# Causal attention and the experts behind it, joined in one block, with one activation-table load moved

## The reference, cut to what matters

```python
qkv = einsum(layernorm(x), qkv_weight)                # 16 heads of 8, 4 key heads
probs = softmax(where(causal, q @ k * scale, min))    # over the 32 positions of the first axis
h = x + (probs @ v) @ proj_weight                     # "hidden_after_attn"
x2 = layernorm(h)
gate = softmax(x2 @ router_weight)                    # 8 experts, top 2 keep their probability
h_mid = gelu(x2 @ moe_w1)                             # for each expert, 256 wide
out = h + sum(weight_e * (h_mid_e @ moe_w2_e))
```

## Time and profile before

| | us |
|---|---|
| median of 3 runs | 852.64 (851.43 to 855.21) |
| the profiled execution, its own time | 857.17 |
| its span (first to last instruction) | 855.3 |
| PE busy | 720.1 (84%) |
| DVE busy | 614.5 (72%) |
| ACT busy | 418.2 (49%) |
| POOL busy | 218.1 (25%) |

### The profile page before, as it was taken

One profiled execution on the slowest core, in us unless ns is written; L12 is line 12 of the kernel. 1 busy time (PEld: TensorE's weight loads), 2 busy tenths in 40 slices (PEclk: granted clock), 3 DMA queues, 4 the chain that ended last, 5 costly groups with the idle time before them and its releaser, 6 DMA issues. The chain is left out here.

```text
span 855.3 us, 25351 instructions
## 1 busy us (share of the span) xinstructions
PE 720.1 (84%) x9696; PEld 526.7 (62%) x9696; DVE 614.5 (72%) x1802; ACT 418.2 (49%) x777; POOL 218.1 (25%) x327
## 2 busy tenths in 40 slices
PE   3459988889797999998996488778759999999997
PEld 2335555555465767776774255556537888888886
DVE  7567887877777888888872688777555666666653
ACT  3022333223243777776664356656425455554553
POOL 3344222332428133431001734331011111011100
PEclk9968999899796999999997699999969999999999
DMA  4000000041035122222200000000000000000000
GB/s 104 9 18 18 23 21 21 23 96 21 12 84 128 54 63 74 74 77 70 82 15 13 0 5 4 5 4 5 4 3 1 14 12 5 8 12 12 12 13 13
DMA packets 33078, 26.36 MB, mean 31 GB/s; under 512 B 9740, under 2 KB 29912, under 8 KB 32984
## 3 DMA queue, kind: packets, MB, share of 16 engines
q1 hardware_dynamic: 29944, 24.07, 10.7%
q10 hardware_dynamic: 3040, 0.98, 0.5%
HBM read 13.51 MB, written 7.34 MB: 24 GB/s over the span
## 5 line engine op out<-in xcount | busy, mean ns | idle before, releaser
L1964 PEld LDWEIGHTS bank<-w2r,hme 128*128 128x128 f32 x1024 | 132.6, 192 | 15.8 <-ACT hme L1909 1.4
L1964 PE MATMUL bank<-w2r,hme 128*128 128x128 f32 x1024 | 135.8, 276 | 0.0
L1909 ACT ACTIVATE hme<-bank,b 128x512 f32<-128x512 f32 x128 | 86.5, 687 | 97.7 <-PE bank L104 97.7
L1933 DVE SCALAR_TENSOR_TENSOR Xq<-bank,wgte,Xq 128x128 f32 (+1 forms) x256 | 72.1, 343 | 52.6 <-PE bank L1964 39.8
L1096 DVE TENSOR_REDUCE mx<-bank 128x4 f32<-128x512 f32 x128 | 87.9, 688 | 24.9 <-PE bank L1141 23.4
L1014 ACT ACTIVATE P<-bank 128x512 f32<-128x512 f32 x128 | 76.5, 600 | 15.3 <-PE bank L1162 14.0
L530 ACT ACTIVATE w2r<-bank 128x512 f32<-128x512 f32 x40 | 23.9, 597 | 115.4 <-PE bank L843 85.2
L1089 DVE TENSOR_SCALAR P<-P 128x512 f32<-128x512 f32 x128 | 61.3, 479 | 3.1 <-ACT P L1014 3.0
L102 PE MATMUL bank<-xTe,w 128*128 (+1 forms) x128 | 49.2, 385 | 5.4 <-PEq L1328 5.4
L1739 POOL TENSOR_SCALAR rs<-mv 128x4 f32<-128x4 f32 x8 | 1.6, 194 | 203.4 <-DVE mv L1801 203.4
L854 PE MATMUL bank<-w_raw,hm 128*128 128x128 f32 x320 | 49.1, 303 | 2.8 <-DVE X L768 2.4
(11 more groups left out here) (384 smaller groups left out, 1779.3 us busy)
## 6 DMA issues: line engine op xcount, KB each, us to landing
cross_q<-qh SPq DMA_DIRECT2D x24, 128.0 KB
Q<-cross_q SPq DMA_DIRECT2D x8, 384.0 KB, 4.1
X<-in_x SPq DMA_DIRECT2D x8, 256.0 KB, 2.8
Xq<-X SPq DMA_DIRECT2D x32, 64.0 KB
cross_k<-kh SPq DMA_DIRECT2D x16, 128.0 KB
Yq<-Y SPq DMA_DIRECT2D x32, 64.0 KB
out_x<-Xq SPq DMA_DIRECT2D x32, 64.0 KB
cload<-in_ctx SPq DMA_DIRECT2D x8, 192.0 KB, 2.6
```

The costliest lines, as they stand in the source:

```text
L1909: act.activation(hm[:, p % HR], UP[p % RING][:], ACT.Gelu_apprx_tanh, bias=b1[:, p:p + 1]).then_inc(s["gelu"], 1)
L1933: last = dve.scalar_tensor_tensor(x, Y[f % 2][:, 128 * i:128 * i + 128], w, x, ALU.mult, ALU.add)
L1964: last = pe.matmul(Y[f % 2][:, cols], hm[:, p % HR, cols], w2r[:, p], start=(p % 2 == 0 and i == 0), stop=(p % 2 == 1), skip_group_check=True)
```

## The change

The two functions `attention2` and `experts1` become one block. `experts` no longer opens a block of its own but returns five functions, which the engines call behind their part of the attention. What the barrier had guaranteed is now said by waits on semaphores of the attention (`t` is the attention's set): PE waits ahead of its first upward product for the last `at_f` (its bank 0 is read by L1552), for the last reads of the other banks, and for the last but one `at_lo`; behind the projection of group 1 it waits for the last `at_lo`. ACT gets one more activation, a gelu of one column (the half of `half2`, written to `Kc`, which nobody reads any more) behind the exponential of the first group, which brings the gelu's table load there. Nothing of what is computed changes.

```diff
-def attention2(nc, d, bank, keep, H, AT, wp, e):
+def attention2_experts(nc, d, bank, keep, H, AT, wp, out, e):
...
+        sync, gpsimd, scalar, vector, tensor = experts(bank, keep, Xq, H, AT, wp, out, e, s)
...
                 expert_root(pool, e, 0)
                 expert_sum(pool, e, Xq, H, 0)
+                gpsimd(pool)
...
                     if q == QUADS + 1:
                         expert_exp(act, e, 0)
+                        act.activation(Kc[:, 0:1], half[:, 0, 0:1], ACT.Gelu_apprx_tanh)
                 for q in range(FIRST, QUADS + 4):
                     step(q)
+                scalar(act)
...
+                vector(dve)
...
+                tensor(pe)
...
-def experts1(nc, d, bank, keep, X3, H, AT, wp, out, e):
+def experts(bank, keep, X3, H, AT, wp, out, e, t):
...
+    def gpsimd(pool):
+        pool.wait_ge(t["summed"], G)
+        pool.wait_ge(t["h_ready"], G)
...
+    def vector(dve):
+        dve.wait_ge(t["h_ready"], G)
...
+    def tensor(pe):
+        pe.wait_ge(keep["w2_in"], 16)
+        pe.wait_ge(t["at_f"], G)
+        pe.wait_ge(t["at_lo"], G - 1)
+        pe.wait_ge(t["dd_inv"], G)
+        pe.wait_ge(t["o_sb"], G)
+        pe.wait_ge(t["p_ready"], 4 * G)
+        pe.wait_ge(t["v_ready"], 4 * G)
+        pe.wait_ge(t["mT_ready"], 4 * G)
+        pe.wait_ge(s["g_in"], 1)
...
+                if nxt(g) and p == 0:
+                    expert_project(pe, e, AT, wp, PX, g + 1)
+                    if isinstance(g, int) and g == 0:
+                        pe.wait_ge(t["at_lo"], G)
...
-        attention2(nc, d, bank, keep, keep["X"], AT, wp, moe)
-        experts1(nc, d, bank, keep, keep["Xq"], keep["X"], AT, wp, out, moe)
+        attention2_experts(nc, d, bank, keep, keep["X"], AT, wp, out, moe)
```

More of the change, by code:

```diff
@@ L1326, in attention2, with _ @@
         FIRST = -12
+        sync, gpsimd, scalar, vector, tensor = experts(bank, keep, Xq, H, AT, wp, out, e, s)
         with nc.Block() as block:
+            @block.sync
+            def _(sp):
+                sync(sp)
             @block.gpsimd
@@ L1877, in late @@
         return (h, (p - lag) % NB) if cur(h) else None
[L1879 to L1927, removed]
-                else:
[L1929 to L1986, removed]
@@ new lines, in sync, with step @@
+    def sync(sp):
+        for g in range(G):
+            sp.wait_ge(s["x4_ready"], g + 1)
+            for i in range(4):
+                at = 32 * i + GB * g
+                sp.dma_start(out[:, at:at + GB, :], X3[32 * i:32 * i + 32, GB * g:GB * g + GB, :]
+                             ).then_inc(s["stored"], 16)
+        sp.wait_ge(s["stored"], 16 * 4 * G)
+    def gpsimd(pool):
+        pool.wait_ge(t["summed"], G)
+        pool.wait_ge(t["h_ready"], G)
+        def step(g):
+            for p in range(NB):
+                if nxt(g) and p == 1:
+                    expert_root(pool, e, g + 1)
+                if nxt(g) and p == 9:
+                    expert_sum(pool, e, X3, H, g + 1)
+        over_rest(pool, step, G - 1)
@@ new lines, in scalar, with step @@
+    def scalar(act):
+        def step(g):
+            for p in range(NB):
+                k = NB * g + p
+                if cur(g):
+                    act.wait_ge(s["up_psum"], k + 1)
+                    after(act, s["down_psum"], k - HR + 1)
+                    act.activation(hm[:, p % HR], UP[p % RING][:], ACT.Gelu_apprx_tanh, bias=b1[:, p:p + 1]
+                                   ).then_inc(s["gelu"], 1)
+                if nxt(g) and p == 6:
+                    expert_high(act, e, PX, g + 1)
+                if nxt(g) and p == 10:
+                    expert_exp(act, e, g + 1)
+        over_rest(act, step, G - 1)
@@ new lines, in vector, with combine, step @@
+    def vector(dve):
+        dve.wait_ge(t["h_ready"], G)
+        def combine(at):
+            if at is None:
+                return
+            g, p = at
+            f = p // 2
+            wait_alone(dve, s["down_psum"], NB * g + p + 1, s["carrier4"])
+            if f == 0:
+                wait_alone(dve, s["r_ready"], g + 1, s["carrier4"])
+            else:
+                wait_alone(dve, s["x4_step"], (NE - 1) * g + f, s["carrier4"])
+            for i in range(GB):
+                x = group(X3, g)[:, i, :]
+                w = group(wgt, g)[:, i, f:f + 1]
+                last = dve.scalar_tensor_tensor(x, Y[f % 2][:, 128 * i:128 * i + 128], w, x, ALU.mult, ALU.add)
+            last.then_inc(s["x4_ready" if f == NE - 1 else "x4_step"], 1)
+        def step(g):
+            for p in range(NB):
+                if p % 2 == 0:
+                    combine(late(g, p, LAG + 1))
+                if nxt(g):
+                    expert_prep(dve, e, H, PX, LG, g + 1, p)
+        over_rest(dve, step, G - 1)
+        for f in (NE - 2, NE - 1):
+            combine((G - 1, 2 * f + 1))
@@ L1989, in causal_tiles @@
+    return sync, gpsimd, scalar, vector, tensor
 def causal_tiles(room):
```

34 lines of the change are left out of this document (added).

## The result

The changed kernel takes 848.44 us (median of 17 runs, 845.01 to 851.87), the kernel before 853.39 (17 runs, 850.16 to 856.22). The ratio is 0.9946, with a 95% interval of 0.9929 to 0.9962: 0.54% less, give or take 0.17%, which is 4.6 us with an interval of 3.2 to 6.1 (the medians differ by 4.95). The forecast was 849.5, within a range of 846.4 to 851.4, and a gain of 3.1 us. The time lies in the range, and the gain is larger than forecast, on the edge of what was called no change.

What follows compares the result with a forecast made beforehand. PE, full through the experts to the end, was taken to bound the kernel, with the barrier's idle time ahead of it. A gain of 4.14 - 1.0 (clock) = 3.1 us from the median 852.64 gave 849.5, range 846.4 to 851.4.

Steps and rivals of the forecast that it cites:

- What bounds the kernel, and the hole: PE is full through the experts to the end; ahead, the barrier idles it 5.44 us without needing the routing's result.
- The barrier goes: 4.14 us: At the border of attention and experts, the product of p = 1 starts at 638.41 instead of 642.55, gaining 4.14 us.
- rival 6: Some wait holds PE's first product until at_lo; gain only 1.6 us, time 851.0; chance 0.05.
- The pause at `at_lo`: Behind the projection of group 1, PE stands still about 0.5 us (1.7 at full clock) for the last at_lo.
- The table load: On ACT behind the routing's exponential, the load's new place and the added gelu neither gain nor cost anything.
- rival 4: The table load delays ACT's high half and thus the wait at at_lo; 0.35 us less gain, 849.9; chance 0.03.
- The clock: 1.0 us of loss: Half clock lasts 3.4 to 6.8 us behind the at_lo pause, costing 1.0 us more, between 0.15 and 1.85.
- rival 2: The at_lo pause is too short to matter to the clock; gain 3.8 to 5.5 us, about 848.0; chance 0.20.
- What follows: DVE's norm for group 1 stays in time with at least 0.9 us of room; the shift reaches the end.
- The slower side: Loop code no longer stays loaded; reloads in six passes cost 7 to 11 us, time 856.5 to 860; chance 0.05.
- The rivals with 851.0: Gain only 1.6 us: an issue pause in the new dense stretch (chance 0.06), or first product held until at_lo (0.05).
- rival 1: The forecast itself, for the border of attention and experts: gain 2.3 to 4.0 us, 848.6 to 850.3; chance 0.43.

Runs made afterwards that it cites:

- e2_load_only: The kernel before, barrier kept, with only the added one-column gelu that brings the table load forward; ratio to the kernel before 1.0006.
- e1_no_early_load: The changed kernel without the added one-column gelu, so the table load falls back ahead of the first real gelu; ratio to the kernel before 0.9945.
- e3_at_lo_first: The changed kernel with PE's wait for the last at_lo moved ahead of its first upward product; ratio to the kernel before 0.9986.
- e6_at_lo_early: The changed kernel with the routing's comparison (steps 12 and 13) moved on DVE behind the last low half; ratio to the kernel before 0.9955.
- e7_gap_filled: The changed kernel with the routing's comparison moved behind the last low half and 6 unused matmuls on PE behind the widening; ratio to the kernel before 0.9946.
- e8_both_gaps_filled: The changed kernel with the routing's comparison moved, and unused PE matmuls, 6 ahead of the last widening and 7 behind; ratio to the kernel before 0.9949.
- e4_wait_routing: The changed kernel, without barrier, but PE waits for DVE's last routing copy ahead of its first upward product; ratio to the kernel before 0.9998.
- e9_at_lo_between: The changed kernel with only step 13 of the routing moved on DVE behind the last low half; ratio to the kernel before 0.9949.
- e11_changed_again: The changed kernel measured once more, unaltered, beside its variants on one chip; ratio to the kernel before 0.9964.
- e10_between_filled: The changed kernel with only routing step 13 moved behind the last low half, plus 6 and 7 unused PE matmuls around the widening; ratio 0.9942.
- e5_border_filled: The kernel before, barrier kept, with 42 unused matmuls of 128 columns on PE behind its last widening; ratio to the kernel before 0.9983.

## Why the prediction was right, and where it was off

**What bounds the kernel, and the hole.** Right. PE stays full from 640 to 840 us, and from the transpose to the end it is 203.8 us before and 203.7 after, so what is won at the border arrives at the end: profiles with and without the barrier differ at the transpose by 4.9 us (17.97 and 17.20 on one side; 12.73, 13.36 and 11.93 on the other; means 17.59 and 12.67), and the medians of the first measurement by 4.95.

**The barrier goes: 4.14 us.** Right in size: 4.13 between the two profiles, 4.14 between e2_load_only and e1_no_early_load (8.60 and 4.46). `at_lo` and not the waits ahead of the first product is what limits p = 1. e3_at_lo_first shows it from the other side: with the two pieces of work behind `at_lo` instead of ahead, p = 1 comes at 7.45. That is the kernel of rival 6, and its gain of 1.54 us up to p = 1 is close to the 1.6 given there. The pause at `at_lo` was to be 0.5 us. The profile counts 0.27, by a modelled end; by the starts, which the prediction went by, it is 2.99 - 2.52 = 0.47. The pause ahead of p = 0 was 0.83 for the 0.8 forecast.

**The table load: nothing.** Right, by e1 and e2. L1442 was to run from about 2.3 to 3.0 us behind the widening's start (635.9 to 636.6) and ran from 2.18 to 2.89. The gap between load and next activation was 0.01 us again (633.30 and 633.31), so the drain that the Trainium skill adds ("ScalarE: Activation LUTs", What ACT_TABLE_LOAD costs) isn't there in this kernel; rival 4's wait for the high half shows only in another order of DVE's work, that of e6_at_lo_early, e7_gap_filled and e8_both_gaps_filled, where DVE waits 0.69 to 1.09 us for it.

**The clock: 1.0 us of loss.** This is the term that failed, in its sign. I took it that the pause at `at_lo` puts the rise off and that half clock lasts 3.4 to 6.8 us behind it. The prediction named a rise sooner than 3.4 us behind the pause as what would show it wrong, and so it came in all three profiles with that pause: half clock lasted 0.87, 2.98 and 0.08 us, 1.3 on the mean, against 3.11 and 2.32 behind the same point in the two with the barrier, 2.7 on the mean. Half of the difference is 0.7 us of gain, and 4.14 + 0.7 is 4.8 us, near the 4.9 of the transposes. That is nearer to rival 2, to which I gave 0.20: a pause of this length didn't put the rise off, and where p = 0 started sooner without filling, the clock rose sooner, 4.5 to 7.4 us behind the widening's start against 10.4 to 12.1. The other runs agree. Behind the start of p = 1, half clock lasted 2.91 and 3.46 us in e3_at_lo_first and e4_wait_routing, which start late as with the barrier, and 2.35 and 1.49 in e6_at_lo_early and e9_at_lo_between, which start early and have no pause. The sizes scatter by 3 us between profiles of one kernel, so 0.7 is rough, and what set the rise within the 3.1 to 6.0 us behind p = 0 stays open. Rival 2's own lower bound of 3.4 us from p = 0 failed once as well, with 3.1. The times alone couldn't tell 3.1 us of gain from 4.8: the intervals are 3.2 to 6.1 us and, in e11_changed_again, 1.4 to 4.9.

The row that misled me was the half clock from 260 to 277 us with pauses of 0.6: it showed that the clock stayed down, and I read from it why. The pauses there come again and again, and the one at `at_lo` comes once; whether that is the difference wasn't tried.

**What follows.** Right: DVE's norm was in time (L1803 at 637.06, and PE's transpose waits for nothing). The room was to be at least 0.9 us: from the end of the norm to the transpose it was 643.97 - 642.65 = 1.32 in the changed profile and 0.92 in e11_changed_again, and e8_both_gaps_filled used it up.

**The slower side.** One pass of the loop still moves only the stores in DMA, and no pause shows in 200 us of PE. The rivals with 851.0 are out as well: PE's first product starts 0.10 us after `Af`. The pauses of rows 7, by which the prediction judged how code is loaded, the profile puts down to issue; no run looked into them, so they show nothing about the loading of code.

**Luck in the number.** The clock's term had the wrong sign, and the time still lies 1.1 us from the forecast. Two things helped: the range took in the rivals, and the forecast was counted from a median of three runs, 852.64, where 17 runs give 853.39. Against the kernel before as it was measured, 3.1 us were forecast and 4.95 came by the medians, outside the 2.3 to 4.0 of my own rival 1; the second measurement, in e11_changed_again, has 851.35 - 848.61 = 2.7. Only the barrier's 4.14 us was hit for its reason.

The reading against the median held: the profiled executions were 3.8 us above and 1.0 above their medians (857.17 against 853.39, 849.45 against 848.44), and most of that lies ahead of the border: behind the widening the two spans differ by 5.3 us, ahead of it by 2.3.

## What to carry to other kernels

Where a barrier stands in front of an engine that is full from there to the end, look up which engine ends last before it and whether the full one needs that result; here it did not. Of the 4.13 us by which p = 1 came forward, 2.59 were work that it could do ahead of the true dependence, about 1.1 the shorter wait, and 0.44 the barrier's own handshake. Take the price of a clock from several profiles, since its rise varied between them by 3 us, and don't read a cause into one row: here one short pause didn't put the rise off. Follow a gain to the end of the span: e10_between_filled won 0.5 us at the transpose against e11_changed_again and lost it behind. A load or a wait that is free behind another engine's work is free only in that order: check it again when that work is moved.

## What the runs showed of the hardware that was not expected

The granted clock rose between 3.1 and 6.0 us behind the experts' first matmul in the profiles in which it was at half there and PE had not been filled (3.9, 6.0 and 3.1 us in the three with a pause of 0.27 us in between; 5.6, 4.8, 5.4, 6.0, 4.9 and 4.0 without it): the pause made no visible difference. After it had risen under the filling of e5_border_filled, 1.94 us without work were followed by a fall while PE was working again. Why it stayed at half from 260 to 277 us in the kernel before stays open; it wasn't tried.
